# Some DMA transposes of an attention front moved to TensorE, and one VectorE step moved ahead of another

## The reference

```python
query = ctx @ Wq.T + bq;  key = ctx @ Wk.T + bk            # (4, 512, 128)
attention = softmax(query @ key.T, axis=-1)                # (4, 512, 512), per batch
x = x + layernorm(x) @ attention.T                         # first layer norm has no weights
v = bf16(layernorm(x));  h = bf16(layernorm(v) * ln_w + ln_b)
h = bf16(mx_quant(h) @ mx_quant(W1).T + b1)                # W1 (2048, 512)
h = bf16(gelu_tanh(h))
h = bf16(mx_quant(h) @ mx_quant(W2).T + b2)                # W2 (512, 2048)
out = x + bf16(v + h)
```

## Time and profile before

| | us |
|---|---|
| runs shown | 278.34, 278.35, 279.96 |
| median | 278.35 |
| profiled execution, own time | 281.02 |
| its span, first to last instruction | 279.2 |
| outside the span (281.02 - 279.2) | 1.8 |
| PE / DVE / ACT / POOL busy in the span | 231.1 / 245.4 / 170.8 / 69.0 |
| mean granted TensorE clock | 0.936 of full |

### The profile page before, as it was taken

How to read it: one execution, slowest core, us unless ns; L and a number is a source line. 1 busy time by engine, 2 the same in 40 slices (tenths; PEclk the granted TensorE clock), 3 DMA queues, 4 the chain that set the end, 5 groups by cost and what they waited for, 6 DMA issues and landing times.

```text
span 279.2 us, 3196 instructions
## 1 busy us (share of the span) xinstructions
PE 231.1 (83%) x946; PEld 99.0 (35%) x946; DVE 245.4 (88%) x361; ACT 170.8 (61%) x287; POOL 69.0 (25%) x100
## 2 busy tenths in 40 slices
PE   7767569981899575919979697999999789999993
PEld 7323324440344132403434233344444334444431
DVE  3488999996579999999979999999999999877992
ACT  2357147437698567834997979956556554565510
POOL 2058210032002330064030020192123333333400
PEclk9979779997599998886999899999999999999998
DMA  5967999999999995969032225456532555555673
GB/s 164 377 250 160 235 161 245 211 214 241 241 254 205 248 150 97 240 123 181 2 61 53 45 49 96 94 115 150 131 68 65 132 132 132 132 132 115 144 180 127
DMA packets 103077, 42.92 MB, mean 154 GB/s; under 512 B 93844, under 2 KB 96152, under 8 KB 102552
## 3 DMA queue, kind: packets, MB, share of 16 engines
q1 hardware_dynamic: 100224, 35.93, 60.5%
q10 hardware_dynamic: 2360, 6.83, 9.8%
q0 software_dynamic: 480, 0.02, 0.1%
HBM read 15.48 MB, written 4.19 MB: 70 GB/s over the span
## 4 chain that ended last, share of the span: by engine, by line
DVE 52%; PE 17%; ACT 9%; DMA 7%; SPq 5%; POOL 4%; issue 4%; POOLq 0%; DVEq 0%; ACTq 0%
DVE amax L805 14%; PE ps L764 9%; PE ps L754 5%; DVE w_int L848 4%; DVE pf L912 4%; DVE wquant L902 4%; SPq L245 3%; DMA xhl<-pf 3%; DVE vw L995 3%; DVE hq L1000 3%; DMA wst<-in_L_ffn_W 3%; DVE phl L983 3%; DVE wquant L907 3%; DVE stats L959 2%; DVE xhl L988 2%
## 5 line engine op out<-in xcount | busy, mean ns | idle before, releaser
L764 PE MATMUL ps<-w2T,xhl 128*128 128x512 bf16 x256 | 57.9, 379 | 4.8 <-DMA xhl<-pf 4.8
L754 PE MATMUL ps<-w1T,cxT 128*128 128x512 bf16 x256 | 59.7, 388 | 0.0
L586 ACT ACTIVATE wst<-ps 128x1024 bf16<-128x1024 f32 x32 | 31.9, 1017 | 23.9 <-PE ps L754 23.9
L805 DVE TENSOR_REDUCE amax<-phl 128x64 f32<-128x2048 bf16 x16 | 36.5, 2280 | 4.1 <-ACT phl L593 4.1
L703 PE MATMUL ps<-pT,xT 128*128 128x512 f16 x96 | 27.0, 441 | 13.5 <-DMA pT<-phl 13.5
L764 PEld LDWEIGHTS ps<-w2T,xhl 128*128 128x128 bf16 x256 | 24.5, 98 | 36.1 <-DMA xhl<-pf 7.3
L754 PEld LDWEIGHTS ps<-w1T,cxT 128*128 128x128 bf16 x256 | 24.2, 100 | 33.8 <-issue 8.3
L593 ACT ACTIVATE phl<-wst 128x2048 bf16<-128x2048 bf16 x16 | 30.6, 1910 | 1.6 <-DVE wquant L902 0.5
L691 PE MATMUL ps<-qkT 128*128 128x512 f32 x32 | 19.4, 720 | 12.8 <-ACT pf L479 6.7
L703 PE MATMUL ps<-h1q,xT 128*128 128x512 f16 x96 | 25.0, 417 | 4.4 <-ACT xs L507 2.9
L445 POOL TENSOR_TENSOR wst<-wst,vs 128x512 bf16<-128x512 bf16 x12 | 15.4, 1284 | 51.0 <-DVE wquant L907 51.0
(11 more groups left out here) (81 smaller groups left out, 368.5 us busy)
## 6 DMA issues: line engine op xcount, KB each, us to landing
wst<-in_L_ffn_W ACTq DMA_DIRECT2D x6, 1024.0 KB, 7.0
xs<-in_x SPq DMA_DIRECT2D x4, 1024.0 KB, 10.1
out_x<-wst SPq DMA_DIRECT2D x16, 256.0 KB, 2.9
cx<-in_ctx SPq DMA_DIRECT2D x4, 512.0 KB, 6.9
wst<-in_L_ffn_W SPq DMA_DIRECT2D x2, 1024.0 KB, 9.7
xhl<-pf SPq DMA_TRANSPOSE x17, 4.3
xT<-xhl SPq DMA_TRANSPOSE x16, 4.4
lnw<-in_L_ffn_ln_w ACTq DMA_DIRECT2D x1, 256.0 KB, 6.0
```

Of the source, the lines that this page charges most:

```text
L586: act.activation(ys[:, k, 1024 * g:1024 * g + 1024], ps_y[:, 2 * g:2 * g + 2, :], ACT.Copy)\
L754: last = pe.matmul(ps_y[:, c, :], h1T[:, k, t, :], w1T[:, 4 * c:4 * c + 4, t, :], start=False, stop=(t == KT - 1))
L764: last = pe.matmul(ps_z[:, k, :], h2T[:, k, t, :], w2T[:, t, :], start=False, stop=(t == FT - 1))
L805: dve.tensor_reduce(amax[:, a, :], by_block, AX_X, ALU.max, apply_absolute_value=True)\
```

## The change

Twelve DMA transposes of 128 x 1024 and one of 128 x 2048 go: the four of x and the four of p of batch 0, the four of x of batch 1, and that of W1's first unit (128 x 2048). PE does them in their place, as 128 x 128 transposes of 16-bit data into PSUM (8 to a tile, 16 for the unit of W1), and ACT copies each tile out in one instruction (16-bit PSUM to 16-bit SBUF). Batch 0's tiles are turned in banks 6 and 7, batch 1's x in banks 2 and 3, W1's unit in banks 0 and 1. Batch 0's front on ACT and PE gets an order of its own (`first_batch` and the lines in its place on PE); in ACT's `batch` for b = 0 a copy `x_turned(t)` follows each x_plus, and `w1_turned` stands ahead of load_w1. queries_keys(2) waits until all four x_turned are done, because it writes the same banks. SP issues the load of x of batch 2 right behind that of context 2. In DVE's `front`, for every batch, p_low of the last tile stands ahead of `w_over(W1, b)`, and the low half and scaled reciprocal of tile 3 stand ahead of p_low of tile 2. DVE also makes two 16-bit copies of the 128 x 128 identity at its start. The mathematics is the same.

```diff
+        W1_BY_PE = 1
+        X_BY_PE = 2
...
+        ps_t = ps[:, 6:8, :].rearrange("p a n -> p (a n)").bitcast(F16).rearrange("p (a c n) -> p a c n", a=2, n=P)
+        ps_xt = ps[:, 2:4, :].rearrange("p a n -> p (a n)").bitcast(F16).rearrange("p (a c n) -> p a c n", a=2, n=P)
+        ps_wt = ps[:, 0:2, :].rearrange("p a n -> p (a n)").bitcast(BF16).rearrange("p (c n) -> p c n", n=P)
...
             def front(b, ctx=None, later=None):
-                x_transpose(b, 0)
+                if b >= X_BY_PE:
+                    x_transpose(b, 0)
...
             load_ctx(2)
-            front(0, None, 2)
+            load_x(2)
             front(1, 3, 3)
...
             def x_high(b, t):
                 act.wait_ge(rsr[0], b + 1)
-                wait(act, xT_rdy[t], 16 * b)
+                if b == X_BY_PE:
+                    act.wait_ge(xt_ps, t + 1)
+                wait(act, xT_rdy[t], 16 * (b - X_BY_PE))
...
+            def turned(n, out):
+                act.wait_ge(t_ps, n + 1)
+                act.activation(out, ps_t[:, n % 2, :, :], ACT.Copy).then_inc(t_sb, 1)
+            def x_turned(t):
+                act.wait_ge(xt_ps, t + 1)
+                act.activation(xT[:, t, :, :], ps_xt[:, t % 2, :, :], ACT.Copy).then_inc(xt_sb, 1)
+            def w1_turned():
+                act.wait_ge(wt_ps, 1)
+                act.activation(w1T[:, 0:4, :, :].rearrange("p r k f -> p (r k) f"), ps_wt, ACT.Copy)\
+                   .then_inc(wt_sb, 1)
+            def first_batch():
+                for t in range(LT + 1):
+                    if t < NT:
+                        exp(0, t)
+                        x_high(0, t)
+                    if t > 0:
+                        p_high(0, t - 1)
+                        turned((0, 1, 3, 5)[t - 1], xT[:, t - 1, :, :])
+                    if t > 1:
+                        turned((2, 4, 6)[t - 2], pTs[0][:, t - 2, :, :])
+                    if t == 2:
+                        context(1)
+                load_w1(1)
+                query_key(1, 0)
+                query_key(1, 1)
+                turned(7, pTs[0][:, NT - 1, :, :])
+                exp(1, 0)
+                x_high(1, 0)
             def batch(b, front, qk, v):
...
+                        if b == 0:
+                            x_turned(t - 2)
+                    if b == 0 and t == LT:
+                        w1_turned()
...
                 if front + 1 < B:
                     load_w1(front + 1)
...
+                x_plus(b, LT - 1)
+                if b == 0:
+                    x_turned(LT - 1)
...
             def values(b, t):
+                if b == 0:
+                    pe.wait_ge(t_sb, 2 * LT)
...
+            def turn(n, source):
+                wait(pe, t_sb, n - 1)
+                for c in range(2 * NT):
+                    last = pe.transpose(ps_t[:, n % 2, c, :], source[:, P * c:P * c + P], ident_h[:, :])
+                last.then_inc(t_ps, 1)
+            def turn_x(t):
+                pe.wait_ge(x_lo, t + 1)
+                turn((0, 1, 3, 5)[t], xhl[:, t, :, :].rearrange("p a n -> p (a n)"))
+            def turn_p(t):
+                pe.wait_ge(p_lo, t + 1)
+                turn((2, 4, 6, 7)[t], phl[:, t, :, :].rearrange("p a n -> p (a n)"))
+            def turn_next_x(t):
+                pe.wait_ge(x_lo, LT + (t + 1))
+                wait(pe, xt_sb, t - 1)
+                for c in range(2 * NT):
+                    last = pe.transpose(ps_xt[:, t % 2, c, :], xhl[:, t, c // NT, P * (c % NT):P * (c % NT) + P],
+                                        ident_h[:, :])
+                last.then_inc(xt_ps, 1)
+            def turn_w1():
+                pe.wait_ge(c_idb, 1)
+                pe.wait_ge(cT_sb, 3)
+                pe.wait_ge(w_step[W1], W_STEPS)
+                for c in range(4 * KT):
+                    last = pe.transpose(ps_wt[:, c, :], wquant[:, W1, P * c:P * c + P], ident_b[:, :])
+                last.then_inc(wt_ps, 1)
             def batch(b, front, qk):
+                if qk is not None:
+                    if b == 1:
+                        pe.wait_ge(wt_sb, 1)
                     context(qk)
                 for t in range(LT):
                     if t < NT - 2:
                         energies(front, t + 2)
+                    values(b, t)
+                    if b == 0:
+                        turn_next_x(t)
+                        if t == 2:
+                            turn_w1()
                 if qk is not None:
+                    if b == 0:
+                        pe.wait_ge(xt_sb, LT)
                     queries_keys(qk)
...
-            batch(None, 0, 1)
+            energies(0, 2)
+            pe.wait_ge(c_idh, 1)
+            turn_x(0)
+            energies(0, 3)
+            turn_x(1)
+            turn_p(0)
+            context(1)
+            turn_x(2)
+            turn_p(1)
+            turn_x(3)
+            turn_p(2)
+            queries_keys(1)
+            turn_p(3)
+            energies(1, 0)
+            energies(1, 1)
             pe.wait_ge(c_idx, 1)
             batch(0, 1, 2)
...
             def w_mult(a, u):
-                wait(dve, (w1T_rdy, w2T_rdy)[a], 16 * u)
+                if a == W1:
+                    if u > 0:
+                        dve.wait_ge(wt_ps, 1)
+                    wait(dve, w1T_rdy, 16 * (u - W1_BY_PE))
+                else:
+                    wait(dve, w2T_rdy, 16 * u)
...
                 recip(b, 3)
+                x_low(b, 3)
+                recip_scaled(b, 3)
                 p_low(b, 2)
-                recip_scaled(b, 3)
-                x_low(b, 3)
+                p_low(b, NT - 1)
                 w_over(W1, b)
-                p_low(b, NT - 1)
                 w_clip(W1, b)
...
+            dve.wait_ge(c_id, 1)
+            dve.tensor_copy(ident_h[:, :], ident[:, :]).then_inc(c_idh, 1)
+            dve.tensor_copy(ident_b[:, :], ident[:, :]).then_inc(c_idb, 1)
```

56 lines of the change are left out of this document (30 added, 26 removed).

## The result

The changed kernel takes **288.24 us** (median of 4 runs, 287.50 to 289.26) against 278.64 for the kernel before on the same chip: a ratio of 1.0337, with a 95% interval of 1.0286 to 1.0389. It is slower, by 9.6 us, where 286.9 was predicted. The profiled execution of the changed kernel took 287.65, its span is 285.8.

What follows compares the result with a forecast made beforehand. DVE and PE were taken as full in the attention half, with a hole between. Front 0's 4.3, PE's 5.2 and front 2's -1.0 gave +8.5 us on the 278.35 median: 286.9, range 281.8 to 290.5.

Steps and rivals of the forecast that it cites:

- signs of being wrong: DVE reaching negmax(2, 0) without a wait, PE waiting for batch 1's p transposes, or front 2's clip shifting unlike the end.
- Step 1: Front 0: five ACT copies of 0.92 us and DVE's reorder move W1's first clip from 29.67 to 33.95, +4.3 us.
- rival of cheap copies: 16-bit ACT copies cost 0.5 us and PE transposes 0.055: only +4.7, 283.0 us; chance 0.15.
- Step 2: PE, 37.8 to 59.6 us: added transposes and a 2.1 us wait for x_turned put negmax(2, 0) at +9.5, 70.5.
- T = 3.5: Price in us of forty added PE transposes before values(0, 3) ends, taken as the middle of 2.2 to 5.2.
- Step 3: Batch 1: values(1, 0) stops waiting for p's DMA transposes; ACT regains only 2.92 us, so p_high(2, 3) moves +6.6.
- the hole: Between 61.0 and 93.7 us: three DVE waits, 2.36, 0.48 and 4.03, together 6.87 us, the most an emptier queue returns.
- the rival in which the change frees nothing: Batch 1's p transposes still land late, values(1, 0) waits two or three us past 73: 287 to 288; chance 0.05.
- The term of -2.92: ACT's idle 2.92 us before x_plus(1, 0) goes, taken off the shift of +9.5.
- the queue worth 6.87 us: All of DVE's three waits come back, PE's transposes vanish between products, only front 0's 4.3 is paid: 275.8; chance 0.12.
- Step 4: Front 2: p_low(2, 3), now ahead of w_over, waits for ACT; the reorder adds 1.9, clip at 95.7, +8.5 us.
- the clock's rival: PE pauses around x_turned and in front 0 drop batch 0's values or queries to 1.2 GHz: 4.9 more, 291.8; chance 0.08.

Runs made afterwards that it cites:

- second profile: The kernel before, unchanged, run once more under the profiler: 279.30 us in one run, beside 278.77; span 277.5.

## Why the prediction was right, and where it wasn't

The direction and the size came out: +8.5 by the sum, +9.6 by the medians. That the size came so close is in good part luck. The 8.5 was made against a profile that took 2.7 more than the median, the terms for PE's stretch came out 3.3 too high and those for front 2 3.1 too low, and the tail wasn't in the sum at all. One of my signs of being wrong did appear: the clip of front 2 moved by 7.4 and the end by 8.3. Two smaller slips: the middle of 2.2 and 5.2 is 3.7, not 3.5, and the sum's upper bound is 278.35 + 10.7 = 289.1, so that the 290.5 of the range, said to lie below it, lies above.

**Step 1, front 0: the mechanism right, the size a little high.** The copies take 1.00 to 1.07 us each and 0.90 to 0.91 from start to start; I had put 0.92. ACT's timeline:

```profile
20.87 1.00 ACT L555 ACTIVATE xT<-ps 128x1024 f16<-128x1024 f16 x1
...
24.57 1.02 ACT L555 ACTIVATE h1q<-ps 128x1024 f16<-128x1024 f16 x1
...
30.07 0.76 ACT L499 ACTIVATE phl<-pf,rinv 128x512 f16<-128x512 f32 x1
```

p_high(0, 3) was forecast for 30.34 and stands at 30.07; the clip was forecast for 33.95 and stands at 33.84. Part of this agreement is the first maximum, which stands 0.40 later than in the profile of before; from there front 0 grew by 3.8 against that profile and 3.1 against the second, where I had 4.3. Nor did the first copy wait for PE, which I had put at 0.35: it starts at 20.87 right behind p_high(0, 0). The share of the order is 1.15 by the run with the old order, against my 2.2. In that run w_over doesn't run beside all of the copies, as I had it, but starts at 29.03, since p_low(0, 2) ahead of it waits for ACT until 27.64. The rival of cheap copies falls with these rows. (By the Trainium skill's "ScalarE: Activation LUTs", section "What ACT_TABLE_LOAD costs", the same copy is 0.95 as an estimate, at one rate for float32 and bf16; the trace, 0.91 from start to start, agrees with it for float16 sources as well.)

**Step 2: the wait right, T mis-sized, the clock missing.** The wait for x_turned was put at 2.1; from the last group of transposes to queries_keys(2) lie 1.95 (59.87 to 61.82), and with late tiles these are gone. "T = 3.5" is the term that failed: eight transposes take 0.45 from start to start (46.38 to 46.83), sixteen 0.89 (55.53 to 56.42), so the forty are 3 x 0.45 + 0.89 = 2.24 us. That is the lower bound that I had given and not chosen. And one term was not in the sum: energies(1, 2) and the first value tile took 3.88 instead of 6.20 in the second profile of before and 5.45 in the first (1.13 + 2.75, 2.08 + 4.12, 1.36 + 4.09). I had looked at the clock for losses only; here it gave back 2.3, or 1.6 against the first profile. It isn't the shorter wait alone that did it: PE waited 2.19 here, 2.34 in the first profile, and only 1.44 and then 0.39 in the run with batch 1's x by PE, whose clock was 0.71 all the same. What sorts the thirteen profiles is batch 0: in the four kernels that turn it on PE the clock over these instructions is 1.00, in the nine that leave it to the DMA 0.56 to 0.71. In the first four PE has the transposes and, up to 36 us, batch 1's queries to do in what is mostly a pause in the others. That this is the reason is argued, not shown. The stretch from energies(1, 2) to energies(2, 0) is 24.33 against 22.46: 4.2 added, 2.3 given back. So negmax(2, 0) came at 67.46 with a wait of 1.81, not at 70.5 with 5.0.

**Step 3: the chain right, the hole not.** I had written that DVE's 2.36 and 0.48 are hidden ACT time and that only 2.92 of ACT comes back. Against the profile that I had, this held: p_low(2, 0) moved by 6.4 (70.41 to 76.84), p_high(2, 3) by 3.4 (85.54 to 88.94), which is 6.4 less the 2.92. values(1, 0) starts at 69.98 behind energies(2, 2), with no wait for p's transposes, so the rival in which the change frees nothing is out as well. But the kernel hardly has that hole: in the second profile of before, ACT goes from v_out to p_high(2, 3) in the same 14.84 us as in the changed kernel. The term of -2.92 took off something that, of all profiles here, only the first had lost. The other rival, the queue worth 6.87 us, fell with it: neither the run with batch 1's x on PE and nothing waiting for it (280.34) nor the one with batch 0 on PE (281.89) beat the kernel before. The transposes by DMA aren't free of cost, though. In two of the nine profiles with batch 0 by DMA its first values waited more than 1 us for p (1.08 with the reorder alone, 2.00 in the slowest run of the version with the context late), and the stretch to negmax(2, 0) was 33.3 and 33.7 us instead of 31.4 to 31.7.

**Step 4, the reorder in front 2: right.** It was forecast at 1.9 us; it costs 2.07, and the old order gets 3.9 back over the whole kernel by the medians. Without any copies on ACT it costs the same. The 0.1 for fronts 1 and 3 is near enough for DVE's own clips (0.35 in either, and nothing at the last scaled reciprocal), and wrong for what front 3 triggers in its trace, which comes next.

**Not foreseen: the tail.** From the last scaled reciprocal to the second amax the changed kernel needs 37.5 us against 36.4. PE's timeline, the changed kernel and then the second profile of before (the first line is the last product of values(3, 2)):

```profile
144.36 1.02 PE L767 MATMUL ps<-xs,ident_x 128*128 128x512 f32 x2
149.00 0.40 PE L860 MATMUL ps<-b1row,ones 3*128 3x512 bf16 x4 [3.62 <-ACT wst L641]
149.32 5.31 PE L865 MATMUL ps<-w1T,cxT 128*128 128x512 bf16 x16
```

```profile
139.25 1.02 PE L706 MATMUL ps<-xs,ident_x 128*128 128x512 f32 x2
141.86 0.40 PE L749 MATMUL ps<-b1row,ones 3*128 3x512 bf16 x4 [1.59 <-ACT wst L586]
142.19 3.63 PE L754 MATMUL ps<-w1T,cxT 128*128 128x512 bf16 x16
```

and the windows of the changed kernel behind that wait (columns as in the earlier trace rows):

```profile
149.00:150.50 1.50, 1.50 (x9) 0.65 (x10) 0.20 (x1) 1.48 (x3) 1.20 (x4) 0.88 0.03 8
150.50:153.00 2.50, 2.50 (x7) 0.91 (x6) 1.94 (x3) 2.49 (x3) 0.49 (x1) 0.50 1.12 212
```

PE waits for ACT's first copy of y, starts, and is then granted 1.2 GHz for 2.5 us. The split over all profiles is clean: waits of 1.56 to 2.46 us were followed by products at full clock and a distance of 36.4 (both profiles of before and the runs with the old order in front 3 and no wait for x_turned), waits of 2.64 to 3.93 by cold products and 37.5 to 38.9. All of the latter have the new order in front 3 or that wait. ACT isn't later in them: counted from the last scaled reciprocal, its first copy of y starts at 23.7 in the changed kernel (146.93) and at 24.0 in the second profile of before (139.80). PE is earlier: its last product of values(3, 2) starts at 21.2 against 23.5. The new order lets the last p_low start 0.9 behind the reciprocal instead of 2.9, so that values(3, 0) starts at 5.8 instead of 7.4, and the time that PE gains it waits out, and then pays for in clock. All five profiles with the new order in front 3 have these distances (values(3, 0) at 5.8 to 5.9, the copy at 23.7), the run with the reorder there alone among them, and none of the other eight has (7.3 to 7.4, and 24.0 to 24.1); so the order is their cause. The old-order run with the wait for x_turned (2.81) is early by shorter value tiles instead, which I can't explain. "PE pauses no longer than it did", my reason against the clock's rival, holds for the attention half and fails here; its price was 1 us and not 4.9.

**The sum again.** Against the second profile: 0.3 (the start) + 3.1 + 1.9 + 2.1 + 1.1 - 0.2 = 8.3 by the traces. Mine was 4.3 + 5.2 - 1.0 = 8.5. Front 0 was too dear by 1.2 (0.5 against the profile that I had); the middle too dear by 3.3, T and the clock; front 2 too cheap by 3.1, mostly the 2.92 of the hole; the tail was left out. By medians, from experiments on several chips: reorder 3.9, the wait for x_turned with the transposes in front of it 2.8, batch 0 by PE 1.5 in this company (2.9 alone), and 1.4 not tried by itself. These parts needn't add up: the table shows that the order and the copies depend on each other.

**The rule for transposes.** The Trainium skill ("VectorE: DVE Perf Modes", sections "The three transpose paths" and "Rules for kernel authors") sends such a transpose to TensorE. The transpose itself is cheap by the rows, 0.056 us each in a row. What decided here was the rest: the copy on ACT at 0.91 per tile, and the places that transposes and copies take in the order of two engines that are on the path. The wait for the DMA that went was worth less: the 1.41 us of values(1, 0) in the second profile never reached DVE.
